# First layer's attention cut from 128x128 squares to the 64x64 blocks of single graphs

## The reference, cut to what matters

```python
# layer 0: B = 128 graphs, N = 64 nodes, D = 256, H = 4 heads of hd = 64
x1 = relu(layernorm((L_norm @ x) @ Wc + bc)) + x
q, k, v = (x1 @ W).reshape(B, N, H, hd).transpose(0, 2, 1, 3)   # for Wq, Wk, Wv
scores = jnp.einsum('bhnd,bhmd->bhnm', q, k) / np.sqrt(hd)
scores = jnp.where(adjacency[None, None] > 0, scores, -1e9)
attn = jax.nn.softmax(scores, axis=-1)
o = jnp.einsum('bhnm,bhmd->bhnd', attn, v) ; o = o.transpose(0, 2, 1, 3).reshape(B, N, D)
x2 = layernorm(x1 + o @ Wo + bo)
out = layernorm(x2 + gelu(x2 @ W1 + b1) @ W2 + b2)
```

## Time and profile before

| | |
|---|---|
| median of three runs | 2377.62 us (2375.21 to 2378.91) |
| the profiled execution | 2375.64 us |
| its span in the trace | 2373.8 us |
| TensorE busy over the span | 93% |
| VectorE, ScalarE, GpSimd busy | 61%, 52%, 20% |
| first layer's main loop, first to last matmul | from 41 us to 713 us |

### The profile page before, as it was taken

How to read it: one execution, slowest core, us unless ns; L and a number is a source line. 1 busy time by engine, 2 the same in 40 slices (tenths; PEclk the granted TensorE clock), 3 DMA queues, 4 the chain that set the end, 5 groups by cost and what they waited for, 6 DMA issues and landing times. The chain is left out here.

```text
span 2373.8 us, 37509 instructions
## 1 busy us (share of the span) xinstructions
PE 2219.3 (93%) x13775; PEld 1977.9 (83%) x13775; DVE 1444.6 (61%) x2733; ACT 1235.8 (52%) x2295; POOL 477.0 (20%) x906
## 2 busy tenths in 40 slices
PE   5999999999996999999999999999999797979997
PEld 4988888988886998888888889988888797968886
DVE  4888888888884554443334343344443677856775
ACT  1544454454452346754444344354433575968887
POOL 3244334333430000000000000000000221016665
PEclk9999999999998999999999999999999898989999
DMA  3110110111003211000000000000000331011221
GB/s 96 32 54 17 37 53 22 35 49 53 13 28 102 61 39 36 18 1 18 1 1 18 18 1 1 1 1 1 1 1 1 108 118 58 1 31 59 74 71 49
DMA packets 76393, 81.72 MB, mean 34 GB/s; under 512 B 6544, under 2 KB 74000, under 8 KB 75408
## 3 DMA queue, kind: packets, MB, share of 16 engines
q1 hardware_dynamic: 76304, 80.51, 10.9%
HBM read 55.33 MB, written 25.17 MB: 34 GB/s over the span
## 5 line engine op out<-in xcount | busy, mean ns | idle before, releaser
L298 PE MATMUL ps<-R 128*128 128x256 f32 (+3 forms) x8520 | 1489.5, 335 | 30.1 <-DVE R L1480 14.1
L298 PEld LDWEIGHTS ps<-R 128*128 128x128 f32 x8520 | 1326.9, 190 | 174.9 <-DVE R L1480 14.3
L1174 ACT ACTIVATE late_half<-ps,lstm_bias 128x512 f32<-128x512 f32 (+2 forms) x460 | 283.1, 669 | 381.6 <-PE ps L298 381.6
L340 POOL TENSOR_TENSOR ln_veps<-ln_mv,eps_tile 128x2 f32<-128x2 f32 x128 | 28.3, 221 | 1277.3 <-DVE ln_mv L323 1277.3
L812 PE MATMUL ps<-H 128*128 128x256 f32 x1024 | 237.6, 381 | 3.0 <-ACT H L734 1.7
L812 PEld LDWEIGHTS ps<-H 128*128 128x128 f32 x1024 | 188.9, 191 | 26.2 <-ACT H L734 1.9
L1209 DVE TENSOR_TENSOR late_half<-late_half 128x1024 f32<-128x1024 f32 (+2 forms) x32 | 37.6, 1176 | 186.3 <-ACT late_half L1174 186.3
L1171 ACT ACTIVATE late_half<-late_half 128x1024 f32<-128x1024 f32 (+2 forms) x66 | 68.1, 1032 | 124.5 <-DVE late_half L1214 78.5
L1211 DVE TENSOR_TENSOR late_half<-late_half 128x1024 f32<-128x1024 f32 (+2 forms) x32 | 37.6, 1176 | 132.4 <-ACT late_half L1174 132.4
L366 DVE SCALAR_TENSOR_TENSOR H<-H,ln_rstd 128x256 f32<-128x256 f32 x192 | 100.2, 563 | 6.7 <-POOL ln_rstd L333 3.2
L1218 DVE TENSOR_TENSOR H<-late_half 128x1024 f32<-128x1024 f32 (+2 forms) x34 | 45.9, 1349 | 89.1 <-ACT late_half L1174 89.1
(11 more groups left out here) (209 smaller groups left out, 3031.0 us busy)
## 6 DMA issues: line engine op xcount, KB each, us to landing
H<-in_x SPq DMA_DIRECT2D x64, 256.0 KB, 4.2
residual<-H SPq DMA_DIRECT2D x32, 256.0 KB, 2.2
H<-residual SPq DMA_DIRECT2D x32, 256.0 KB, 3.0
arena<-residual SPq DMA_DIRECT2D x32, 256.0 KB, 2.7
residual<-arena SPq DMA_DIRECT2D x32, 256.0 KB, 2.2
H_state<-residual SPq DMA_DIRECT2D x32, 256.0 KB, 2.7
out<-H_state SPq DMA_DIRECT2D x32, 256.0 KB, 2.2
arena<-in_wih SPq DMA_DIRECT2D x4, 1024.0 KB, 4.9
```

The lines of the kernel that those rows point to most:

```text
L298: mm = pe.matmul(out, lhsT(a), rhs(b), start=start and n == 0, stop=stop and n == len(PASSES) - 1)
L1174: ins = act.activation(into[q][:, m, 0:x.cols], gate_ps(q, m, x.cols), ACT.Tanh if q == TANH_G else ACT.Sigmoid, bias=lstm_bias[:, x.p - 1 ...
```

## The change

Scores are kept only for pairs within a graph, as 64x64 blocks. Both graphs of a tile lie on the partitions (rows are queries, 64 for each graph), the columns are the 64 keys of the own graph. One head and tile so takes 64 columns where it took 128.

- The mask is 64 columns wide; `far` (other graph) is no longer added for it, one operation less in the setup on GpSimd. The two mask matmuls write 256 columns each where they wrote 512.
- Scores: 16 products (32 records) of 64 rows by 64 columns of the array on 64 columns, where there were 8 (16 records) of 64 by 128 on 128 columns. `f` picks the half of the array's rows (head), `graph_rows(g)` the half of its columns (graph).
- To have a graph's queries side by side, the transposes of x1 write their columns ordered by graph (`by_graph`); `product_by_graph` makes the values with one graph of each of the two tiles together, with the same 12 matmuls.
- DVE's maxima, sums and scaling, and ACT's eight exponentials, work on half the elements.
- Four transposes instead of eight: a transpose turns a head of both tiles at once (`attn_pairs`), so ACT's copy has 512 columns instead of 1024.
- Values: 16 products (32 records), 64 keys deep, 64 rows high, on 64 columns, where there were 8 (16 records), 128 deep, 64 high, on 128 columns. A semaphore increment (`alone`) stands ahead of them. The copy after them reads two banks.

```diff
-            link(pool.tensor_scalar(masked, adj_bd, 0.0, -NEG, ALU.is_le, ALU.mult))
-            link(pool.tensor_tensor(mask0[:], far, masked, ALU.add))
+            link(pool.tensor_scalar(mask0[:], adj2, 0.0, -NEG, ALU.is_le, ALU.mult))
...
+    def score_blocks(s):
+        return ps[:, BANKS * s:BANKS * (s + 1), 0:NJ * NODES].rearrange("p b (c k) -> p b c k", k=NODES)
...
                     for j in range(2 * NJ):
-                        ins = act.activation(attn_bd[s][:, j, :], squares(s)[:, j, :], ACT.Exp,
+                        ins = act.activation(attn[s][:, j, :], score_blocks(s)[:, j // NJ, j % NJ, :], ACT.Exp,
                                              bias=sm_max[:, s, j:j + 1])
...
-                    act.activation(attnT[s], squares(s), ACT.Copy).then_inc(atT_ready[s], 1)
+                    act.activation(attnT[s], squares(s)[:, 0:HEADS, :], ACT.Copy).then_inc(atT_ready[s], 1)
...
-                    dve.tensor_reduce(sm_max[:, s, :], squares(s), AX_X, ALU.max, negate=True).then_inc(sc_ready[s], 1)
+                    dve.tensor_reduce(sm_max[:, s, :].rearrange("p (b c) -> p b c", b=2), score_blocks(s), AX_X,
+                                      ALU.max, negate=True).then_inc(sc_ready[s], 1)
...
-                    for g in range(2):
-                        pe.matmul(squares(s)[:, g * NJ:(g + 1) * NJ, :], ident_r[:],
-                                  mask0[:].unsqueeze(1).to_broadcast([P, NJ, P]),
+                    for h1 in range(2):
+                        pe.matmul(score_blocks(s)[:, h1], ident_r[:],
+                                  mask0[:].unsqueeze(1).to_broadcast([P, NJ, NODES]),
                                   start=True, stop=False, skip_group_check=True)
-                    for n in range(TILES):
-                        q = slice(n * P, (n + 1) * P)
-                        for h2 in range(HEADS // 2):
+                    for h2 in range(HEADS // 2):
+                        for n in range(TILES):
+                            c = TILES * h2 + n
                             for g in range(2):
-                                f = slice(HEAD_DIM * g, HEAD_DIM * (g + 1))
-                                mm = pe.matmul(squares(s)[:, g * NJ + 2 * n + h2, :], qkT[s][f, 0, h2, q],
-                                               qkT[s][f, 1, h2, q], start=False,
-                                               stop=n == TILES - 1 and h2 == HEADS // 2 - 1, skip_group_check=True)
+                                q = slice(g * P + NODES * n, g * P + NODES * (n + 1))
+                                for h1 in range(2):
+                                    f = slice(HEAD_DIM * h1, HEAD_DIM * (h1 + 1))
+                                    mm = pe.matmul(score_blocks(s)[graph_rows(g), h1, c, :], qkT[s][f, 0, h2, q],
+                                                   qkT[s][f, 1, h2, q], start=False, stop=c == NJ - 1,
+                                                   skip_group_check=True)
...
-                    for j in range(HEADS * TILES):
-                        mm = pe.transpose(squares(s)[:, j, :], attn_bd[s][:, j, :], ident[:])
+                    for j in range(HEADS):
+                        mm = pe.transpose(squares(s)[:, j, :], attn_pairs[s][:, j, :], ident[:])
...
-                    for n in range(TILES):
-                        for h in range(HEADS):
-                            g, h2 = h % 2, h // 2
-                            mm = pe.matmul(feature_major(s, 1)[HEAD_DIM * g:HEAD_DIM * (g + 1), h2,
-                                                               n * P:(n + 1) * P],
-                                           v_t[s][:, n, HEAD_DIM * h:HEAD_DIM * (h + 1)],
-                                           attnT[s][:, g * NJ + 2 * n + h2, :], start=True, stop=True)
+                    alone(pe, waits_passed)
+                    for h2 in range(HEADS // 2):
+                        for g in range(2):
+                            for n in range(TILES):
+                                keys = slice(NODES * n, NODES * (n + 1))
+                                for h1 in range(2):
+                                    h = 2 * h2 + h1
+                                    mm = pe.matmul(mixed_rows(s)[HEAD_DIM * h1:HEAD_DIM * (h1 + 1), n, h2, graph_rows(g)],
+                                                   v_t[s][keys, g, HEAD_DIM * h:HEAD_DIM * (h + 1)],
+                                                   attnT[s][keys, 2 * h1 + h2, graph_rows(g)],
+                                                   start=True, stop=True)
```

More of the change, by code:

```diff
@@ L158, in build_program @@
     ahatT = sb("ahatT", [P, P])
-    mask0 = ctx.enter_context(nc.sbuf_tensor("mask0", [P, P], F32R))
+    mask0 = ctx.enter_context(nc.sbuf_tensor("mask0", [P, NODES], F32R))
     bias3 = ctx.enter_context(nc.sbuf_tensor("bias3", [P, 2, P], F32R))
@@ L610, in build_program @@
     xr0, zt_words, hbuf, x1, vt, x1b, x2b = ([buf(G2) for _ in S] for _ in range(7))
-    attn_bd = [buf(HEADS * TILES, P) for _ in S]
-    attnT = [buf(HEADS * TILES, P) for _ in S]
+    attn = [buf(HEADS * TILES, NODES) for _ in S]
+    attn_pairs = [v.rearrange("p (h n) k -> p h (n k)", n=TILES) for v in attn]
     xs_t, xr0_t, hb_t, x1_t, v_t, x1b_t, x2b_t = ([tiles_of(v) for v in b]
@@ L617, in build_program, with mixed_rows, by_graph, graph_rows @@
     fm = [w0r(2, KD, GROUP) for _ in S]
-    flat_at = [v.rearrange("p a b -> p (a b)") for v in attnT]
+    flat_at = [buf(HEADS * TILES * P) for _ in S]
+    attnT = [v[:, 0:HEADS * P].rearrange("p (h q) -> p h q", h=HEADS) for v in flat_at]
     qkT = [v.rearrange("p (q k n) -> p q k n", q=2, k=KD) for v in flat_at]
     mT = [v.rearrange("p (m n) -> p m n", m=HID0 // P) for v in flat_at]
+    def score_blocks(s):
+        return ps[:, BANKS * s:BANKS * (s + 1), 0:NJ * NODES].rearrange("p b (c k) -> p b c k", k=NODES)
+    def mixed_rows(s):
+        return ps[:, BANKS * s:BANKS * (s + 1), 0:KD * P].rearrange("p n (k q) -> p n k q", k=KD)
+    def by_graph(v):
+        return v.rearrange("p k (g n i) -> p k n g i", g=2, n=TILES)
+    def graph_rows(g):
+        return slice(NODES * g, NODES * (g + 1))
     def up_ps(s):
@@ L723, in stage @@
                     act.wait_ge(turned[s], 3 * turn + 2)
-                    act.activation(attnT[s], squares(s), ACT.Copy).then_inc(atT_ready[s], 1)
+                    act.activation(attnT[s], squares(s)[:, 0:HEADS, :], ACT.Copy).then_inc(atT_ready[s], 1)
                 if slot == 10:
                     act.wait_ge(mixed[s], 2 * turn + 2)
-                    act.activation(zT_f[s], feature_major(s, 1), ACT.Copy).then_inc(mixed_ready[s], 1)
+                    act.activation(zT_f[s].rearrange("p k (n q) -> p n k q", n=TILES), mixed_rows(s),
+                                   ACT.Copy).then_inc(mixed_ready[s], 1)
                 if slot == 13:
@@ L778, in stage @@
                     c.settle()
-                    dve.tensor_tensor(attn_bd[s], attn_bd[s], sm_inv[:, s, :].unsqueeze(2).to_broadcast([P, 2 * NJ, P]),
+                    dve.tensor_tensor(attn[s], attn[s], sm_inv[:, s, :].unsqueeze(2).to_broadcast([P, 2 * NJ, NODES]),
                                       ALU.mult).then_inc(at_ready[s], 1)
@@ L814, in product, with product_by_graph @@
                 return mm
-            def exact_product(out, src, w):
-                for n in range(TILES):
+            def product_by_graph(out, src, w):
+                for g in range(2):
                     for k in range(KD):
-                        mm = exact_mm(pe, out[:, n, :], lambda q: src[:, q, k, n * P:(n + 1) * P],
+                        mm = exact_mm(pe, out[:, g, :], lambda q: src[:, q, k, g * P:(g + 1) * P],
                                       lambda q: w[:, q, k, :], k == 0, k == KD - 1)
@@ L834, in turn_over, with by_tile @@
                     for k in range(KD):
-                        mm = pe.transpose(out[:, k, n * P:(n + 1) * P], src[:, n, k * P:(k + 1) * P], ident[:])
+                        mm = pe.transpose(out[:, k, n], src[:, n, k * P:(k + 1) * P], ident[:])
                 return mm
+            def by_tile(v):
+                return v.rearrange("p k (n q) -> p k n q", n=TILES)
             def stage(s, slot, turn):
@@ L851, in stage @@
                     pe.wait_ge(x_ready[s], 2 * turn + 1)
-                    turn_over(feature_major(s, 0), x1_t[s]).then_inc(turned[s], 1)
+                    turn_over(by_graph(feature_major(s, 0)), x1_t[s]).then_inc(turned[s], 1)
                 if slot == 4:
@@ L894, in stage @@
                     pe.wait_ge(x_ready[s], 2 * turn + 2)
-                    turn_over(feature_major(s, 1), hb_t[s]).then_inc(turned[s], 1)
+                    turn_over(by_tile(feature_major(s, 1)), hb_t[s]).then_inc(turned[s], 1)
                 if slot == 14:
```

4 lines of the change are left out of this document (2 added, 2 removed).

## The result

The changed kernel takes 2340.05 us (median of four runs, 2337.86 to 2342.6), the kernel before 2377.12 us in the same comparison: 37.1 us less, a ratio of 0.9845 with a 95% interval of 0.9834 to 0.9857. Forecast were 2342 us.

What follows compares the result with a forecast made beforehand. TensorE and VectorE were both taken as close to the bound, each holding parts of a turn. Savings of 1.4, 2.1, 1.2 and 0 make 4.7 us, 37.6 over 8 turns, taken as 36: 2342 us, range 2328 to 2363.

Steps and rivals of the forecast that it cites:

- All four parts: A turn of the first layer's loop, cut where one engine waits for another: saves 1.4, 2.1, 1.2 and 0 us.
- the last one: From 368.60 us to the next turn's L768: VectorE is busy and none of its operations shrinks, so 0 saved.
- A sum over TensorE alone: TensorE's shorter mask, score, transpose and value stages in the first layer's loop: 1.45 us a group, 5.8 a turn.
- the part that TensorE holds: From 342.17 to 368.60 us: TensorE runs through; two value stages and one set of transposes save 1.2 us.
- that four quarters work at once: Score and value stages: all four quarters share a slot of half the length, 8 slots of 0.055 us.
- The saving of 0.40 a stage: Score and value stages on TensorE: each 0.40 us shorter per group, 0.44 less a bit for the filling.
- The bound on the other side: Score and value stages: quarters don't overlap beyond two, each loses 0.88 us; 17 us slower, 2395 us; chance of slower 0.07.
- The prediction's densest place: Score and value stages: no denser place than 55 ns a record, cited for the rival that intake of records limits them.
- the fastest rival: First layer's loop: TensorE's waits shrink instead of grow, 50 to 60 us gained, 2320 to 2328 us; more than 46: 0.08.
- The first part: L768 at 315.04 to L768 at 327.10 us: VectorE holds it; shorter exponentials, L775 and L779 save 1.4 us.
- The collision: First part: VectorE's L779 takes 2.29 us instead of 1.22 beside GpSimd's addition L688; ending earlier hands this to the next operation.
- the discount for the first and last turn: First layer's loop: the first turn fills the pipeline and the last drains, so 36 us taken in place of 37.6.

Runs made afterwards that it cites:

- the late norm: Changed kernel with the third normalisation's affine step moved from tick 104 to 109 and its followers 5 ticks later; 2328.71 us, 48.6 less than the kernel before.
- the scores alone: Kernel before with only the score products run as 16 on quarters of the array; 2373.24 us.
- half the softmax: Kernel before with maxima, exponentials, sums and scaling on the first 64 of 128 columns of each square, TensorE's work unchanged; 2366.21 us.
- TensorE's share alone: Changed kernel with VectorE's and ScalarE's attention work at the old size; 2389.12 us, or 2372.51 us with the other buffers at the changed kernel's addresses.
- the values alone: Kernel before with only the value products as 16 on quarters, the semaphore increment ahead and a copy reading two banks; 2371.08 us.
- The pairs: Changed kernel with score and value products reordered so that only two quarters can work at once; 2348.17 us.

## Why the prediction was right

**The parts.** The forecast rested on cutting the turn where one engine waits for the other and asking, part by part, whose work counts. All four parts came out, the last one to a hundredth of a microsecond: the mask and score stage in it is 0.7 us shorter on TensorE (1.79 to 1.10 us from first start to last end), and all of that went into the wait for the split (0.98 to 1.67 us), since VectorE's chain fills this stretch and is unchanged. (It was not as full of work as the prediction took it: 2.1 us of it are L366 beside two additions, which the late norm gave back.) A sum over TensorE alone, 5.8 us a turn, would have given 46 us. The runs with one share of the change agree: the scores alone gave 4.8 us (forecast 4), half the softmax 2.1 us a turn (forecast 1.6), and the two shares apart are worth 3.5 us a turn against 5.0 together. They also show where the parts are too simple: TensorE's share alone gave 1.4 us a turn and not 2.2, and the values alone 0.9 and not 1.2, since in the part that TensorE holds VectorE is close behind. In the whole change VectorE's operations shrink too, and that part gave its 1.2.

**The quarters.** The one step without a row behind it, that four quarters work at once, held: 0.52 us for a score stage that the forecast put at 1.09 - 0.40 = 0.69. The saving of 0.40 a stage was too low for the scores with value products behind them (0.57) and near for the values (0.29 to 0.44); the sum of the two, 0.80, measured about 0.95. The bound on the other side was wrong: it gave a quarter the slot of a half, 0.11 us for two records, though a record now has half the columns, and so priced two quarters at a time at 0.88 us more a stage and 17 us slower in all. The pairs measured 29.1 us faster, with rounds of 58 ns. The prediction's densest place, 55 ns a record, was a mean as well: the two records of a round in the kernel before start 7 ns apart. The Trainium skill's floor of 25 ns between starts ("TensorE: Matmul & The Clock Gate", the section on the wait of 56 ns) does not bind between quarters: 7 ns are seen within a round, 15 in the mean. Some 4 ns between tiles, in Part 3 of the same page, is nearer to the 7.

**A reading that was off.** TensorE's fifth wait in a turn is 0.35 us on the weight load ahead of L835; its matmul waits 0.15. The waits of the matmuls add up to 4.1 us a turn and not 4.3. Only the fastest rival used this sum.

**Sizes that were off.** The first part gave 1.65 and not 1.4. The collision moved on as forecast, from the scaling to L366 at 310.02 (1.78 us for two that take 0.88 elsewhere), but cost 0.90 there where it had cost 1.07; and I had taken 0.06 off for it. The exponentials gave the 0.4: the wait's end came 6.10 us after L784 where it came 6.53 after L768, of which 0.43 is theirs. TensorE's wait for L784 fell to 0.41, where I expected 0.9: partly that, and partly a wait of 0.31 us for ScalarE's copy of the keys (L727) that the shorter score stage opened and that I had not seen coming, as little as that of 0.25 for the values' copy (L730). They cost nothing, since VectorE holds these parts.

**The loop and the rest.** The main loop of the first layer, first to last matmul, took 674.21 - 42.39 = 631.8 us where it took 712.95 - 41.43 = 671.5: 39.7 us less, above the 37.6 of the sum, so the discount for the first and last turn was not needed. The median gained 37.1. That 36 came so near is partly luck: the loop gained 4 us more than that, and some of it was lost again elsewhere, 6.6 us in the two profiled executions. Of these, 1.0 lie ahead of the loop, 1.2 in the wait for the second layer's first transfer (20.15 and 21.36 us), 1.3 in the recurrent layer, and 2.4 in TensorE's second wait behind it (6.13 and 8.57 us). The two traces of the pairs, the same kernel twice, differ by 1.9 us in this last wait and by 1.5 in the recurrent layer. What of the loss belongs to the change was not settled.

## What to carry to other kernels

Before pricing a change to two engines that feed each other, mark in the trace the places where one waits for the other, and count each saving only in the parts that its engine holds; the rest turns into a longer wait. A part in which one engine is only just ahead changes hands when that engine alone gets faster. Write small matmuls on disjoint quarters of the array in an order in which four neighbours use four quarters; two at a time cost 8 of the 37 us here. When the waits that stay all point at one engine's unchanged stretch, look in it for an operation that takes longer than elsewhere, and reorder the stretch: moving one stage behind another that TensorE waits for, and with it two GpSimd additions off VectorE's path, gave 11 us more here.

## What was not expected of the hardware

- Moving the buffers by changing the size of small tables made the same program slower by 10 to 15 us at the same mean clock, 10.5 us of it in matmuls of a layer that the change does not touch (961.6 against 951.1 us).
- The granted clock fell to half for 3.4 us at a time behind waits of 1.67 and 1.77 us in some turns of one kernel, and did not behind waits as long in its other turns or in the changed kernel.
- Matmul records of 64 rows, 64 columns of the array and 64 moving columns start 7 ns apart on different quarters, and a quarter takes its next one after 58 ns; with 128 columns on halves it was 112 ns.
- Two VectorE operations of 0.88 us together took 2.97 beside two GpSimd additions (L366).
